# DLRM tower on one core: second layer with samples on partitions, last layer summed along rows by VectorE, narrow products in three of four tiles

## The chip, the core and the metric
One core of a Trainium2 chip. The metric is the device time of one execution in microseconds, as the median of several runs. A measurement of this kernel can tell about 2% from no change.

## What is computed
512 samples. Each has 27 feature vectors of 128 numbers: one dense vector and one row out of each of 26 tables. All 351 products of two different features are formed, and a small network follows.

```python
e = stack([tbl_f[ids[:, f]] for f in range(26)], axis=1)      # tables of 1000 to 125000 rows
all_emb = concatenate([bottom[:, None, :], e], axis=1)        # 512 x 27 x 128
gram = einsum('bfd,bgd->bfg', all_emb, all_emb)
h = concatenate([gram[:, TRIU_I, TRIU_J], bottom], axis=1)    # 351 + 128 = 479 columns
h = maximum(h @ W_top1 + b_top1, 0)                           # 479 -> 512
h = maximum(h @ W_top2 + b_top2, 0)                           # 512 -> 256
y = h @ W_top3                                                # 256 -> 1
```

## The kernel before
The batch is four tiles of 128 samples, a tile being 32 quads of 4 samples. Every engine runs through one list, `PLAN` (line 129), in order, and semaphores tie the engines together.

**Lookups.** The ten smallest tables are looked up by matmul. VectorE (`make_one_hot`, line 632) and ScalarE (lines 696, 703) build one-hot columns for chunks of 125 rows, and TensorE multiplies the table, split in a high and a low part, by them (lines 426, 428). VectorE compares against ids that TensorE has spread over the partitions (`spread_ids`, line 401) into a pair of PSUM banks; ScalarE reads its ids from an SBUF tile that SyncE fills by a broadcast DMA of 256 KB a table (`load_scalar_ids`, line 361). Fillers on the identity matrix (`WARM_UPS`, lines 554, 559) stand ahead of the first table and behind the first spreading. `lookup_ps` is banks 6 and 7.

**Gathers.** The other 16 tables are fetched by 64 indirect DMAs that GpSimd issues one after another (line 345). TensorE turns each with a transpose (`turn`, line 438), four to a group; VectorE or ScalarE copy the group into `turned` (line 582). `TURNED_BY_LOOKUP` says which groups are turned behind which table, 0 to 10 in all; groups 11 to 16 are in `LATE_ORDER`.

**Products.** The 17 blocks (8 quads each, the last two 6 and 2) are multiplied by `multiply` (line 442). Tile 0 has blocks 0 to 3, tile 1 blocks 4 to 7, tile 2 blocks 8 to 11, tile 3 blocks 12 to 16. For each quad there are two matmuls, one for a pair of samples: 56 stationary columns (2 x 28 slots) by 52 moving columns; the two pairs write to PSUM rows 0 to 55 and 64 to 119. Two of the four 28 x 26 squares of a pair are wanted, the others are cross products of two samples and are copied along. `keep` (line 586) copies a block to `products`, VectorE the even and ScalarE the odd ones. `products` has two buffers, so the keep of the first block of tile 2 or 3 waits until tile 0 or 1 is stored.

**The way through DRAM.** SyncE's queue stores a part's products by `store_part` (4 DMAs) and reads them back by `load_part` (7 DMAs) as `pairs`, with the pairs on partitions. The order on the queue is store 0, load 0, store 1, load 1 and so on; each store waits for the keeps, each load for its store. In the last part GpSimd and ScalarE take some of both; ScalarE's two loads stand behind its relus of part 2.

**Layers.** A part has 7 outputs, of 128 columns each. Outputs 0 to 3 are the first layer (`add_dense` line 488, then three `add_pairs` matmuls line 494), 4 and 5 the second (`add_hidden1`, line 501, four matmuls each), 6 the last (`y`, line 508, two matmuls with one stationary column). Features are on partitions throughout. VectorE and ScalarE take them in turn (`take_output`, lines 600 to 615). In the first three parts the outputs alternate between banks 6 and 7. Each fp32 matmul appears in the trace as two instructions, a fp32r matmul or a transpose as one.

`LATE_ORDER` is the order behind the lookups: m is the next block multiplied, t the next group turned, o the next output. With the numbers written out it is now m0 to m8, t11, t12, m9 to m12, o0.0, t13, o0.1 to o0.3, m13, o0.4, t14, o0.5, m14, o0.6, o1.0, t15, o1.1 to o1.4, t16, o1.5, m15, m16, o1.6, o2.0 to o2.6. Then part 3 is done by `layers`.

## Time and profile before
| | us |
|---|---|
| median of 3 runs | 116.31 |
| lowest and highest | 114.5, 116.79 |
| the profiled execution | 113.72 |
| its span, first to last instruction | 111.9 |

The profile is of one execution, so durations and starts are of that one; starts count from the start of the span. PE is TensorE's matmuls, PEld its weight loads, DVE VectorE, ACT ScalarE, POOL GpSimd, SP SyncE; a q behind a name is the queue that issues DMAs. A busy TensorE is not one at its peak, since matmuls overlap: the distance between starts tells more than the duration of one. A mean clock of 0.985 of full speed was granted.

### The profile page before, as it was taken

To read this page: it belongs to the slowest core of one execution; us is meant where nothing else is said; L and a number is where in the kernel's file an instruction comes from. 1 tells how busy PE (TensorE), PEld (TensorE's weight loads), DVE (VectorE), ACT (ScalarE), POOL (GpSimd) and SP (SyncE) were. 2 spreads that over 40 slices of the span, in tenths; PEclk is the share of its full clock that TensorE was granted. 3 is DMA by queue.
4 is the path that set the end of the run, shared out by engine and by line. 5 is a ranking of instruction groups with operands and counts; after the bars stand their busy time and mean duration, and the time that the engine had idled before them with its cause. 6 is when DMAs were issued, how large, how long until landed. Compare 5 with 4: busy or idle time off the path is not lost.

```text
span 111.9 us, 2590 instructions
## 1 busy us (share of the span) xinstructions
PE 103.9 (93%) x1000; PEld 83.7 (75%) x1000; DVE 70.0 (63%) x93; ACT 64.7 (58%) x89; POOL 64.7 (58%) x73
## 2 busy tenths in 40 slices
PE   4969999999999999999998989999869999999892
PEld 4945776868686877766684679998769899897890
DVE  1089999997999999999999144653041512312111
ACT  3386999999999997895952056455214132321111
POOL 2677777776877776777767777777763000212000
PEclk9995799999999999999999999999999999999999
DMA  2899999999998978997322122644646110132000
GB/s 43 243 278 250 215 256 251 252 241 278 242 291 180 261 208 234 278 270 192 92 59 47 51 66 53 151 114 103 191 104 183 41 38 0 33 104 52 14 0 1
DMA packets 10237, 16.67 MB, mean 149 GB/s; under 512 B 5091, under 2 KB 5618, under 8 KB 10225
## 3 DMA queue, kind: packets, MB, share of 16 engines
q1 hardware_dynamic: 7648, 12.03, 42.0%
q0 software_dynamic: 2144, 4.30, 15.3%
q10 hardware_dynamic: 433, 0.18, 0.8%
q8 instruction: 8, 0.13, 0.5%
q14 instruction: 4, 0.03, 0.2%
HBM read 15.01 MB, written 1.49 MB: 147 GB/s over the span
## 4 chain that ended last, share of the span: by engine, by line
PE 31%; DVE 23%; issue 13%; DMA 13%; POOL 10%; SPq 5%; ACT 2%; POOLq 0%; ACTq 0%; DVEq 0%
DVE one_hot L632 17%; POOL mixed_sb L345 10%; PE banks L494 9%; PE banks L501 6%; PE banks L456 6%; DVE low L646 5%; DMA mixed_sb<-in_mixed_table,mixed_rows_sb 5%; DMA products_dram<-products 4%; SPq L318 3%; PE banks L488 3%; PE banks L426 2%; SPq L330 2%; DMA starts_sb<-in_starts 2%; PE banks L428 2%; DMA pairs<-products_dram 2%
## 5 line engine op out<-in xcount | busy, mean ns | idle before, releaser
L345 POOL DMA_INDIRECT mixed_sb<-in_mixed_table,mixed_rows_sb x64 | 62.3, 973 | 21.2 <-issue 19.2
L632 DVE TENSOR_SCALAR one_hot<-banks,starts_sb 125x1024 fp32r<-125x1024 f32 (+1 forms) x44 | 43.8, 1036 | 3.8 <-PE banks L401 3.1
L426 PE MATMUL banks<-one_hot,high 125*128 125x512 f32 x68 | 29.5, 433 | 1.6 <-DVE low L646 1.0
L428 PE MATMUL banks<-one_hot,low 125*128 125x512 f32 x68 | 27.6, 406 | 0.0
L426 PEld LDWEIGHTS banks<-one_hot,high 125*128 125x128 f32 x68 | 13.2, 194 | 11.0 <-DVE one_hot L632 4.0
L708 ACT COPY turned<-banks 128x512 f32<-128x512 f32 x10 | 10.7, 1075 | 9.2 <-PE banks L428 9.1
L678 ACT ACTIVATE hidden<-banks,b_sb 128x128 f32<-128x128 f32 x12 | 4.4, 368 | 19.1 <-PE banks L494 12.8
L428 PEld LDWEIGHTS banks<-one_hot,low 125*128 125x128 f32 x68 | 13.3, 195 | 2.2
L620 DVE TENSOR_SCALAR hidden<-banks,b_sb 128x128 f32<-128x128 f32 x12 | 4.2, 348 | 17.1 <-PE banks L494 11.0
L646 DVE TENSOR_TENSOR low<-raw,high 125x512 fp32r<-125x512 f32 (+1 forms) x20 | 14.7, 736 | 0.0
L456 PE MATMUL banks<-turned 128*56 128x52 f32 x512 | 14.3, 215 | 0.5 <-ACT turned L708 0.5
L456 PEld LDWEIGHTS banks<-turned 128*56 128x56 f32 x512 | 13.7, 132 | 1.2 <-issue 0.8
L596 DVE COPY products<-banks 120x416 f32<-120x416 f32 (+1 forms) x9 | 7.4, 824 | 11.1 <-PE banks L456 5.9
L494 PE MATMUL banks<-pairs,w_sb 128*128 128x128 f32 (+2 forms) x96 | 13.0, 276 | 1.1 <-DMA pairs<-products_dram 1.1
L696 ACT ACTIVATE distance<-lookup_ids_sb,starts_sb 125x512 f32<-125x512 int32 x20 | 13.3, 712 | 0.1
L686 ACT CAST high<-raw 125x1024 fp32r<-125x1024 f32 (+2 forms) x11 | 11.5, 1054 | 2.4 <-DMA raw<-in_tbl 2.4
L494 PEld LDWEIGHTS banks<-pairs,w_sb 128*128 128x128 f32 (+2 forms) x96 | 11.7, 191 | 1.4 <-DMA pairs<-products_dram 1.4
L596 ACT COPY products<-banks 120x416 f32<-120x416 f32 (+1 forms) x8 | 7.0, 870 | 7.5 <-PE banks L456 6.0
L703 ACT ACTIVATE scalar_one_hot<-distance 125x1024 fp32r<-125x1024 f32 x10 | 10.6, 1060 | 0.3
L438 PE MATMUL banks<-identity,mixed_sb 128*128 128x128 f32 x64 | 9.6, 274 | 0.2 <-DMA mixed_sb<-in_mixed_table,mixed_rows_sb 0.2
L582 ACT COPY turned<-banks 128x512 f32<-128x512 f32 (+1 forms) x13 | 7.8, 607 | 3.0 <-PE banks L438 3.0
L438 PEld LDWEIGHTS banks<-identity,mixed_sb 128*128 128x128 f32 x64 | 7.7, 141 | 1.7 <-DMA mixed_sb<-in_mixed_table,mixed_rows_sb 0.4
(32 smaller groups left out, 82.0 us busy)
## 6 DMA issues: line engine op xcount, KB each, us to landing
raw<-in_tbl SPq DMA_DIRECT2D x6, 448.0 KB
lookup_ids_sb<-in_lookup_ids SPq DMA_DIRECT2D x10, 256.0 KB, 6.8
raw<-in_tbl SPq DMA_DIRECT2D x4, 560.0 KB
products_dram<-products SPq DMA_DIRECT2D x14, 91.0 KB
mixed_sb<-in_mixed_table,mixed_rows_sb POOLq DMA_INDIRECT x64, 5.7
pairs<-products_dram SPq DMA_DIRECT2D x15, 39.0 KB
w_sb<-in_w SPq DMA_DIRECT2D x2, 256.0 KB
w_sb<-in_w SPq DMA_DIRECT2D x1, 512.0 KB, 13.9
```

The source lines that it names most:

```text
L345: pool.indirect_dma_start(mixed_sb[:, n, :], None, mixed_table, bass.IndirectOffsetOnAxis(ap=mixed_rows_sb[:, n:n + 1], axis=0),).then_inc ...
L426: pe.matmul(lookup_ps[:, i % 2, :], high[0:TABLE_PARTS, i % 2, c, :], columns, start=(c == 0), stop=False)
L428: last = pe.matmul(lookup_ps[:, i % 2, :], low[0:TABLE_PARTS, i % 2, c, :], columns, start=False, stop=(c == CHUNKS_OF[i] - 1))
L438: last = pe.transpose(turn_ps[:, n % 2, k, :], source, identity[:])
L456: last = pe.matmul(product_ps[rows, b % len(PRODUCT_BANKS), k, 0:PAIR * OTHERS], turned[:, t, q, samples, :].rearrange("p j f -> p (j f)") ...
L494: last = pe.matmul(out(n).rearrange("h (j q) -> h j q", j=QUAD), w1_sb[0:rows, c, h * P:(h + 1) * P], pairs[0:rows, p, :, c, :], start=Fal ...
L596: copy(products[:, t % 2, :, :, quads].rearrange("p j g q -> p q (j g)"), product_ps[0:HALF_END, b % len(PRODUCT_BANKS), 0:quads.stop - qu ...
L632: dve.tensor_scalar(one_hot[0:TABLE_PARTS, n % ONE_HOT_RING:n % ONE_HOT_RING + once, :], banks[0:TABLE_PARTS, first:first + once, :], floa ...
L646: dve.tensor_tensor(low[0:TABLE_PARTS, i % 2, chunks, :], raw[0:TABLE_PARTS, i % RAW_RING, chunks, :], high[0:TABLE_PARTS, i % 2, chunks, ...
L686: act.copy(high[0:TABLE_PARTS, i % 2, chunks, :], raw[0:TABLE_PARTS, i % RAW_RING, chunks, :]).then_inc(high_set, 1)
L696: act.activation(distance[0:TABLE_PARTS, k, :], lookup_ids_sb[0:TABLE_PARTS, i % RAW_RING, :], ACT.Square, bias=starts_sb[0:TABLE_PARTS, F ...
L708: act.copy(turned[:, :, :, :, FIRST_LOOKUP + i].rearrange("p t q j -> p t j q"), lookup_ps[:, i % 2, :].rearrange("p (t j q) -> p t j q", ...
```

## The change
- `add_hidden1` is turned round: hidden1 (128 features by 128 samples) is stationary, and all 256 columns of w2 move. One output of 256 columns takes the place of two of 128; samples are on partitions, features along the row. A part has 5 outputs instead of 7.
- The last layer has no matmul any more. VectorE adds b2 along the row (from PSUM), then one `scalar_tensor_tensor` takes the maximum with 0, multiplies by w3 and sums the row into a column of `y_sb`. For that b2 and w3 are loaded broadcast over all partitions. The output is 128 rows of 4.
- Outputs 0, 2 and 4 of a part are VectorE's, 1 and 3 ScalarE's.
- In tiles 0, 2 and 3 each sample of a quad is a matmul of its own: 28 stationary by 26 moving columns, the four samples at PSUM rows 0, 32, 64 and 96. The keep there copies 124 rows of 26 columns a quad instead of 120 rows of 52.
- Fillers: 5 and 4 instead of 8 and 2.
- ScalarE's ids for the first table come from one more spreading matmul in bank 7; their broadcast DMA is gone.
- Group 1 is turned behind table 1, with group 0, instead of behind table 2.
- The new late order, written out: m0 to m4, t11, m5 to m8, t12, m9 to m12, o0.0 to o0.4, t13, o1.0 to o1.3, t14, t15, m13, t16, m14, m15, m16, o1.4, o2.0 to o2.4.

```diff
-WARM_UPS = (8, 2)
+WARM_UPS = (5, 4)
...
+SAMPLE_START = 32
+PRODUCT_ROWS = (QUAD - 1) * SAMPLE_START + SLOTS
+SINGLE_TILES = {0, 2, 3}
...
-LATE_ORDER = "mmmmmmmmmttmmmmotooomotomootooootommoooooooo"
-TURNED_BY_LOOKUP = {1: 0, 2: 2, 3: 3, 4: 4, 5: 5, 6: 6, 7: 7, 8: 8, 9: 10}
+LATE_ORDER = "mmmmmtmmmmtmmmmoooootoooottmtmmmoooooo"
+TURNED_BY_LOOKUP = {1: 1, 2: 2, 3: 3, 4: 4, 5: 5, 6: 6, 7: 7, 8: 8, 9: 10}
...
+def taker(n):
+    return n % OUTS % 2
...
-            load_scalar_ids(0)
...
-            sp.dma_start(w3_sb[:], w3).then_inc(small_in, 16)
+            sp.dma_start(w3_sb[:], w3.to_broadcast([P, HIDDEN2])).then_inc(small_in, 16)
...
-            sp.dma_start(b2_sb[:], b2).then_inc(small_in, 16)
+            sp.dma_start(b2_sb[:], b2.to_broadcast([P, HIDDEN2])).then_inc(small_in, 16)
...
-                    for h in range(HALVES):
+                    for j in range(QUAD) if t in SINGLE_TILES else []:
+                        last = pe.matmul(product_ps[sample_rows(t, j), b % len(PRODUCT_BANKS), k, 0:OTHERS],
+                                         turned[:, t, q, j, :], turned[:, t, q, j, 1:FEATURES],
+                                         start=True, stop=True)
+                    for h in [] if t in SINGLE_TILES else range(HALVES):
...
-                return pe.matmul(out(n), w2_sb[:, c, h * P:(h + 1) * P], hidden1[:, c, 0:width(p)],
+                return pe.matmul(banks[:, bank_of(n), 0:HIDDEN2], hidden1[:, c, :], w2_sb[:, c, :],
                                  start=(c == 0), stop=(c == OUTS1 - 1))
...
+            pe.matmul(lookup_ps[0:TABLE_PARTS, 1, :], ids_rows[:, BATCH:BATCH + 1].to_broadcast([ID_ROWS, TABLE_PARTS]),
+                      ids_rows[:, 0:BATCH], start=True, stop=True).then_inc(first_ids_spread, 1)
...
+            if t in SINGLE_TILES:
+                copy(products[:, t % 2, 0, :, quads].rearrange("p g q -> p q g"),
+                     product_ps[0:PRODUCT_ROWS, b % len(PRODUCT_BANKS), 0:quads.stop - quads.start, 0:OTHERS]
+                     ).then_inc(kept[which], 1)
+                return
...
+            if p >= 1:
+                eng.wait_ge(y_set, p)
+            eng.tensor_tensor(hidden2[:], banks[:, bank_of(n), 0:HIDDEN2], b2_sb[:], ALU.add
+                              ).then_inc(layer_taken[which], 1)
+            eng.wait_ge(layer_taken[which], takes(n))
+            eng.scalar_tensor_tensor(weighted[:], hidden2[:], 0.0, w3_sb[:], ALU.max, ALU.mult,
+                                     accum_out=y_sb[:, p:p + 1]).then_inc(y_set, 1)
...
-    out = nc.dram_tensor("out_y", (1, BATCH), F32, kind="ExternalOutput").ap()
+    out = nc.dram_tensor("out_y", (P, TILES), F32, kind="ExternalOutput").ap()
```

## Rows read from the trace of the kernel before
**Rows 1.** The page: busy time, share of the span and instructions of each engine.
```profile
PE 103.9 (93%) x1000; PEld 83.7 (75%) x1000; DVE 70.0 (63%) x93; ACT 64.7 (58%) x89; POOL 64.7 (58%) x73
```

**Rows 2.** Busy time by stretches (columns: span, busy us PE, PEld, DVE, ACT, POOL; clock, DMA share, GB/s).
```profile
8.95:12.36 3.41, 3.35 (x9) 1.98 (x8) 3.41 (x5) 2.44 (x4) 2.58 (x3) 0.50 1.04 237
...
77.61:82.07 4.46, 2.76 (x24) 2.37 (x20) 1.03 (x2) 1.18 (x3) 3.49 (x4) 1.00 0.49 142
82.07:102.00 19.93, 19.93 (x240) 18.79 (x240) 5.11 (x13) 4.86 (x11) 3.96 (x6) 1.00 0.29 74
```

**Rows 3.** The timeline (start us, duration us, engine, line): product matmuls.
```profile
65.57 7.65 PE L456 MATMUL banks<-turned 128*56 128x52 f32 x288 [0.46 <-ACT turned L708]
```

**Rows 4.** The timeline: SyncE's queue, stores and loads of the parts.
```profile
70.09 1.63 SPq L318 DMA_DIRECT2D products_dram<-products  x4
...
73.58 2.65 SPq L330 DMA_DIRECT2D pairs<-products_dram  x7
```

**Rows 5.** The timeline: what waited between 78 and 83 us, and the last keep.
```profile
78.86 0.94 PE L494 MATMUL banks<-pairs,w_sb 128*128 128x128 f32 x6 [0.76 <-DMA pairs<-products_dram]
...
80.99 0.85 DVE L596 COPY products<-banks 120x416 f32<-120x416 f32 x1 [4.01 <-DMA products_dram<-products]
...
82.07 0.49 PE L488 MATMUL banks<-dense_turned,w_sb 128*128 128x128 f32 x2 [0.94 <-DVE hidden L620]
...
96.05 0.34 DVE L596 COPY products<-banks 120x104 f32<-120x104 f32 x1 [0.62 <-PE banks L456]
```

**Rows 6.** The groups of instructions by line and form (after the bar: busy us, mean ns).
```profile
L456 PEld LDWEIGHTS banks<-turned 128*56 128x56 f32 x512 | 13.7, 132 | 1.2 <-issue 0.8
...
L646 DVE TENSOR_TENSOR low<-raw,high 125x512 fp32r<-125x512 f32 x12 | 8.2, 681 | 0.0
...
L596 DVE COPY products<-banks 120x416 f32<-120x416 f32 x8 | 7.1, 884 | 10.5 <-PE banks L456 5.3 <-DMA products_dram<-products 5.2
L646 DVE TENSOR_TENSOR low<-raw,high 125x640 fp32r<-125x640 f32 x8 | 6.5, 817 | 0.0
...
L494 PEld LDWEIGHTS banks<-pairs,w_sb 128*128 128x128 f32 x32 | 4.8, 191 | 1.4 <-DMA pairs<-products_dram 1.4
...
L620 DVE TENSOR_SCALAR hidden<-banks,b_sb 128x128 f32<-128x128 f32 x12 | 4.2, 348 | 17.1 <-PE banks L494 11.0 <-PE banks L501 6.1
...
L508 PE MATMUL banks<-hidden,w_sb 128*1 128x128 f32 x16 | 2.6, 271 | 0.5 <-ACT hidden L678 0.3
```

**Rows 7.** The timeline: the tail, from the last loads to the output.
```profile
102.23 0.76 ACTq L330 DMA_DIRECT2D pairs<-products_dram  x2
...
102.90 0.97 PEld L488 LDWEIGHTS banks<-dense_turned,w_sb 128*128 128x128 f32 x8 [0.22 <-issue]
...
104.36 2.75 PEld L494 LDWEIGHTS banks<-pairs,w_sb 128*128 128x128 f32 x24 [0.49 <-DMA pairs<-products_dram]
...
109.42 0.60 PE L508 MATMUL banks<-hidden,w_sb 128*1 128x128 f32 x4 [0.33 <-ACT hidden L678]
...
110.34 0.24 SPq L392 DMA_DIRECT2D out_y<-y_sb  x1
```

**Rows 8.** The timeline: the front; the last line is line 345's time to landing.
```profile
5.15 1.35 PE L401 MATMUL banks<-ids_rows 11*125 11x512 f32 x4
...
12.93 0.95 POOL L345 DMA_INDIRECT mixed_sb<-in_mixed_table,mixed_rows_sb  x1 [0.31 <-issue]
...
18.22 0.60 PE L438 MATMUL banks<-identity,mixed_sb 128*128 128x128 f32 x4
...
23.20 0.60 PE L438 MATMUL banks<-identity,mixed_sb 128*128 128x128 f32 x4
...
24.00 0.66 PE L438 MATMUL banks<-identity,mixed_sb 128*128 128x128 f32 x4 [0.20 <-DMA mixed_sb<-in_mixed_table,mixed_rows_sb]
...
26.57 1.28 DVE L632 TENSOR_SCALAR one_hot<-banks,starts_sb 125x1024 fp32r<-125x1024 f32 x1 [0.70 <-PE banks L428]
...
DMA to landing us min/median/max: 2.5/5.7/8.6
```

More of the change, by code:

```diff
@@ L166, in kept_by, with takes @@
     return (blocks + 1 - which) // 2
-def layer_turns(n):
-    return n // 2 + 1
+def taker(n):
+    return n % OUTS % 2
+def takes(n):
+    return [taker(m) for m in range(n + 1)].count(taker(n))
 def bank_of(n):
@@ L388, in _ @@
                 load_part(sp, p, sync_loads(p), pairs_in[p])
-            for which in range(2):
-                n = len(PARTS) * OUTS - 1 - which
-                sp.wait_ge(layer_taken[n % 2], layer_turns(n))
+            sp.wait_ge(y_set, len(PARTS))
             sp.dma_start(out, y_sb[:]).then_inc(y_stored, 16)
@@ L459, in multiply, with out @@
                 last.then_inc(block_multiplied, 1)
-            def out(n, rows=P):
-                return banks[0:rows, bank_of(n), 0:width(n // OUTS)]
+            def out(n):
+                return banks[:, bank_of(n), 0:width(n // OUTS)]
             def open_bank(n):
                 if bank_user(n) is not None:
-                    pe.wait_ge(layer_taken[bank_user(n) % 2], layer_turns(bank_user(n)))
+                    pe.wait_ge(layer_taken[taker(bank_user(n))], takes(bank_user(n)))
                 elif bank_of(n) in TURN_BANKS:
@@ L474, in await_taken @@
             def await_taken(n):
-                pe.wait_ge(layer_taken[n % 2], layer_turns(n))
+                pe.wait_ge(layer_taken[taker(n)], takes(n))
             def await_pairs(p):
@@ L498, in add_hidden1 @@
             def add_hidden1(n, c):
-                p, k = divmod(n, OUTS)
-                h = k - OUTS1
-                return pe.matmul(out(n), w2_sb[:, c, h * P:(h + 1) * P], hidden1[:, c, 0:width(p)],
+                return pe.matmul(banks[:, bank_of(n), 0:HIDDEN2], hidden1[:, c, :], w2_sb[:, c, :],
                                  start=(c == 0), stop=(c == OUTS1 - 1))
-            def y(n):
-                p = n // OUTS
-                for c in range(OUTS2):
-                    await_taken(p * OUTS + OUTS1 + c)
-                    last = pe.matmul(out(n, 1), w3_sb[:, c:c + 1], hidden2[:, c, 0:width(p)],
-                                     start=(c == 0), stop=(c == OUTS2 - 1))
-                return last
             def output(n):
@@ L523, in output @@
                         last = add_hidden1(n, c)
-                else:
-                    last = y(n)
                 last.then_inc(layer_done, 1)
@@ L538, in layers @@
                     add_pairs(n).then_inc(layer_done, 1)
-                for n in range(first + OUTS1, first + OUTS1 + OUTS2):
-                    open_bank(n)
-                    for c in range(OUTS1 - 1):
-                        await_taken(first + c)
-                        add_hidden1(n, c)
-                await_taken(first + OUTS1 - 1)
-                for n in range(first + OUTS1, first + OUTS1 + OUTS2):
-                    add_hidden1(n, OUTS1 - 1).then_inc(layer_done, 1)
-                open_bank(first + OUTS - 1)
-                y(first + OUTS - 1).then_inc(layer_done, 1)
+                n = first + OUTS1
+                open_bank(n)
+                for c in range(OUTS1):
+                    await_taken(first + c)
+                    last = add_hidden1(n, c)
+                last.then_inc(layer_done, 1)
             pe.wait_ge(identity_set, 1)
@@ L595, in keep, with take_output @@
             quads = quads_of(b)
-            copy(products[:, t % 2, :, :, quads].rearrange("p j g q -> p q (j g)"),
+            if t in SINGLE_TILES:
+                copy(products[:, t % 2, 0, :, quads].rearrange("p g q -> p q g"),
+                     product_ps[0:PRODUCT_ROWS, b % len(PRODUCT_BANKS), 0:quads.stop - quads.start, 0:OTHERS]
+                     ).then_inc(kept[which], 1)
+                return
+            copy(products[0:HALF_END, t % 2, :, :, quads].rearrange("p j g q -> p q (j g)"),
                  product_ps[0:HALF_END, b % len(PRODUCT_BANKS), 0:quads.stop - quads.start, 0:PAIR * OTHERS]
                  ).then_inc(kept[which], 1)
-        def take_output(copy, relu, eng, which, n):
-            if n % 2 != which:
+        def take_output(relu, eng, which, n):
+            if taker(n) != which:
                 return
@@ L739, in _ @@
                         act.wait_ge(small_in, 16 * 3)
-                    take_output(act.copy, relu, act, 1, n)
+                    take_output(relu, act, 1, n)
                 else:
@@ L743, in _ @@
                     for k in range(OUTS):
-                        take_output(act.copy, relu, act, 1, n * OUTS + k)
+                        take_output(relu, act, 1, n * OUTS + k)
 def kernel(**inputs):
@@ L789 @@
         arg("starts", starts), arg("w1", w1), arg("b1", columns(inputs["b_top1"])),
-        arg("w2", inputs["W_top2"]), arg("b2", columns(inputs["b_top2"])),
-        arg("w3", columns(inputs["W_top3"])), out)
+        arg("w2", inputs["W_top2"]), arg("b2", np.asarray(inputs["b_top2"]).reshape(1, HIDDEN2)),
+        arg("w3", np.asarray(inputs["W_top3"]).reshape(1, HIDDEN2)), out)
     result = run_bass_kernel_spmd(nc, [arrays], core_ids=[0])
-    return np.asarray(result.results[0]["out_y"]).reshape(BATCH, 1)
+    return np.asarray(result.results[0]["out_y"]).T.reshape(BATCH, 1)
```

51 lines of the change are left out of this document (26 added, 25 removed).

## Prediction
> **What bounds the kernel now.** The page's busy shares come first: TensorE is busy 93% of a 111.9 us span [rows 1]. "Busy" does not yet say that it sets the end, so the chain of waits is read next, and it has three regimes. Until about 64 us it runs through VectorE's one-hot building; TensorE waits for it there and a cheaper matmul would bring nothing. From the first product matmul at 65.57 us to 82.07 us the chain leaves TensorE and goes keep, store, load: the four blocks of tile 0 are multiplied, kept, written out by SyncE's queue and read back [rows 3, 4]. In the table by stretches TensorE is busy for only 2.76 of the 4.46 us from 77.61 to 82.07 us, and fully busy in the 19.93 us after [rows 2]: there every instruction taken off its queue is time. The tail (last pairs at 104.36, end 111.9) is one dependent chain [rows 7].
>
> **Narrow products.** A block of 8 quads is now 32 recorded matmuls. 288 of them, nine blocks, fill 7.65 us [rows 3]: 0.85 us a block, 26 ns each, 104 ns a quad. What makes the 26 ns? A load of 56 columns lasts 132 ns, of 128 columns 191: (191 - 132)/72 = 0.82 ns a column, 46 ns for 56, 105 for 128 [rows 6]. The halves use different columns of the array, so two instructions share a round of 52 ns, which is 46 and a few more. A narrow product loads 28 columns (23 ns) and moves 26 instead of 52. If the four samples' column groups run side by side as the two halves do, a round of four takes about 23 + 6 = 29 ns, and a quad (two rounds, as each fp32 matmul is recorded twice) 58 ns. If an instruction can't follow another in under 26 ns whatever its width, the quad's 8 take 208 ns. The trace has no row with four groups; these are the two ends. I take 60 ns, near the lower end, because load length plus 6 ns explains both spacings of now: 46 + 6 = 52 here, and 105 + 6 = 111 for 128 columns (24 loads in 2.75 us [rows 7], less the last's 0.19, by 23). So a narrow block is 0.48 us, and with the same small waits 0.50, 0.35 less than a wide one. Tiles 0, 2 and 3 have blocks 0 to 3 and 8 to 16.
> The keep copies halve from 416 to 208 columns. VectorE takes 884 ns for 416 and 341 for 104 [rows 5, 6], 1.74 ns a column, so 0.52 us instead of 0.88; ScalarE about the same.
>
> The Trainium skill speaks against this step: TensorE: Matmul & The Clock Gate, section "Wait — 56ns, not 53.3ns?", says that starts never come closer than about 25 ns however few the columns, and the present 26 ns would sit just on that floor; the same page's "Packing small matmuls" has starts in different tiles 4 ns apart. By the first the quad would cost some 200 ns, by the second what I took. No row here separates them.
>
> **Second layer.** Today 16 instructions of 128 moving columns at 0.111 us (1.78 us), then 4 for the last layer (0.60 us with their latency, plus a wait of about 0.2). After: 4 matmuls of 256 columns, 8 recorded instructions. The last layer's one-column weights do not shorten its spacing ((0.60 - 0.27)/3 = 0.11 [rows 6, 7]), so 128 moving columns cost 0.11 and 256 cost 0.22: 8 x 0.22 = 1.75 us. Each part saves about 0.7 us of TensorE. VectorE gets a PSUM addition over 256 columns: 0.35 for the 128-column relu plus 128 x 1.06 ns (from 681 ns at 512 and 817 at 640 columns) = 0.48 us. Then comes a multiply with a row sum: at least 0.68 - 0.27 = 0.41 (the 512-column subtraction less half of its columns) and, if the summing took a pass of its own, 0.85; I take 0.5 [rows 6]. Both are hidden behind other matmuls in parts 0 to 2, where VectorE has 5.11 busy of 19.93 us [rows 2]; in part 3 they are exposed.
>
> **The order after 65.57 us.**
> 1. Blocks 0 to 3 are done 4 x 0.35 = 1.4 us sooner and the last keep is 0.4 shorter. Tile 0's stores start at 68.3 instead of 70.09, the loads land at 77.1 instead of 78.8 [rows 4, 5].
> 2. Nine of the thirteen blocks before the first output are narrow: 9 x 0.35 = 3.1 us, TensorE reaches it at about 74.5 instead of 77.6. But it must wait there for step 1's pairs until 77.1: of 3.1 us, 1.7 arrive.
> 3. VectorE's keep of block 12 stands ahead of its relus and waits until tile 1 is stored; today that holds VectorE 4.01 us and TensorE 0.94 [rows 5]. Those stores are behind tile 0's seven loads on SP (2.65 us [rows 4]), so they too come 1.7 us sooner, at about 79.3, and no more. Output 0.2 starts at about 80.35, not 82.07.
> 4. From there TensorE is the bound. Left: outputs 0.2 and 0.3 and the eight of parts 1 and 2, 10 x 8 x 0.111 = 8.9; three second layers 5.2; turns 13 to 16 (12 transposes and their waits) 1.55; blocks 13 to 16, 24 quads at 0.06 and their waits, 1.6. Sum 17.3, end 97.6; today the queue is there at 102.90 [rows 7], so 5.3 us are gained.
> 5. ScalarE issues its two last loads only after its last relu of part 2. Today they are issued at 102.23 and in use at 104.36 [rows 7]; that relu becomes output 2.3, some 96.5, so they land at 98.6. TensorE's four dense products fill the time until then. The last pairs start at 98.65 instead of 104.36: 5.7 us sooner. The last blocks are kept near 91 instead of 96.4 [rows 5], so the stores are ready before that.
> 6. Tail: pairs 24 x 0.111 = 2.7 (101.35); the relu of the last, 0.25 + 0.35 + 0.1, lies behind the first three second-layer steps (1.3); second layer ends 103.1, visible 103.4; VectorE 0.48 + 0.06 + 0.5 (104.5); the output 1.56 as from 110.34 to 111.9, plus 0.2 for 128 short rows in place of one. End 106.2.
>
> **The front.** Three fewer fillers at first can bring the first spreading of the ids forward (5.15 now [rows 8]), by some tenths. What that gives is lost again: turn 1 now follows table 1. Its last gather starts at 12.93, takes 0.95, lands 5.7 later (median), 19.6 [rows 8]; TensorE is free at 18.66 (four transposes from 18.22) and waits. Table 2 is then delayed by about 1 + 0.45 us and ends at 23.2 + 1.45 = 24.65 (turn 1 starts at 23.20 now); turn 2 follows, done near 25.1 instead of 24.45. VectorE waits for that part of the chain once (0.70 at 26.57 [rows 8]), and its chain sets all until 64 us: 0.5 to 0.65 late. Against this, one 256 KB broadcast is gone, at 237 GB/s 1.1 us of a saturated stream (share 1.04 [rows 2]); the gathers may land up to that much sooner. Together -0.2 to +0.8; I take +0.3. The broadcast w3 and b2 (128 KB each) are wanted 20 us after they are issued, at a DMA share under 0.5: nothing.
>
> **Sum.** 106.2 + 0.3 = 106.5, against a span of 111.9: -5.4 us. The profiled execution took 113.72 us in all, 1.8 around its span, and lies 2.6 under the median of the three, 116.31. I put the difference on the median: 110.9 us.
>
> **Rivals.**
> A (0.12), slower: the narrow matmuls keep 26 ns each. A block is then 1.66 us and more, and the 96 narrow quads, 12 blocks' worth, cost 12 x 0.83 = 10 us more than wide ones. TensorE waits for nothing any more before step 4 (today about 1.7 us), saves 2.1 in the last layer and is through with part 2 at 102.9 + 10 - 1.7 - 2.1 = 109.1; with 0.9 for the dense products, 7.5 for pairs to end and 0 for the front that is a span of 117.5, 121.9 on the median. The floor that the Trainium skill names above would act as this rival. For it: the 26 ns of now; against: the load's length explains the same 26. Between B's 13 ns (109.1) and these 26 (117.5) the end is as before at about 17 ns.
> B (0.13), half of it: the queue delivers an instruction each 13 ns, so a quad costs 104 as now. Step 1 loses 1.4 us, step 4 0.7, and step 2's surplus hides the rest: 106.5 + 2.1 and a few tenths of waits, 109.1, on the median 113.5, 2.4% under before.
> C (0.10), the clock: it stood at half for 3.41 us from 8.95 [rows 2], when TensorE had begun and stopped several times. Step 2 leaves TensorE waiting over 2 us near 75. One such stretch at half speed in step 4 costs 1.7 us: 112.6.
> D (0.05), front: if turn 1 waits for the slowest landing of the trace (8.6 us [rows 8]) it lands at 22.5, 2.9 later than I took: 113.8.
> E (0.05), the transfers do not follow: if tile 1's stores, which cross the gathers, still land at 80.9, step 3's 1.7 us are lost: 112.6.
> The rest, 0.55, is the forecast itself, 108 to 113 with the unknown prices (0.35 for the row sum, 1.0 for the front, the spread of 114.5 to 116.8 in the runs).
>
> **Range and chances.** 107.5 to 115 leaves out A and some 0.03 below and 0.03 between. A measurement of this kernel can tell about 2%, 2.3 us, from no change. Faster by over 2% (below 114.0): the forecast, B for the greater part, C and half of D, 0.75; within: 0.12; slower: A and a trifle, 0.13.
>
> **What would show it.** Spacing of the narrow matmuls: 8 ns or less confirms, 26 is A, 13 is B. Tile 0's stores near 68.3; a TensorE wait of about 2 us for pairs near 75; VectorE's block-12 keep still waiting for tile 1's store; the last pairs starting near 98.9; two VectorE instructions of about 0.5 us at the end; a TensorE wait of 1 us for gathers near 19. Wrong it would be if the instructions that have doubled in number and not their columns set the pace.

## The result, and the profile after

The changed kernel takes 119.36 us (median; 118.99 to 119.91), the kernel before 115.41 us beside it on the same chip: ratio 1.045, interval 1.037 to 1.052. It is slower by 4 us in the medians where 5.4 less were forecast. The ratios with an interval, here and below, compare the fast executions of both kernels alone, and two of the four of the kernel before were slow ones that lift its median. The profiled execution took 118.99 us around a span of 117.2.

The page: busy share of each engine; its row of tenths of the granted clock; the instruction queue (packets, MB, share); and the group of the narrow products (after the bar: busy us, mean ns of one, idle time before them).
```profile
PE 102.3 (87%) x1335; PEld 81.9 (70%) x1335; DVE 69.8 (60%) x99; ACT 60.4 (52%) x83; POOL 63.6 (54%) x73
PEclk9999999999999999999999999999977999999999
q8 instruction: 10, 0.16, 0.5%
L462 PE MATMUL banks<-turned 128*28 128x26 f32 x768 | 10.5, 192 | 7.3 <-issue 6.3
```
[Rows 1] had TensorE busy 93% of 111.9 us. It is now busy 1.6 us less, in a span 5.3 us longer: it stands still more, and what ended the standing is "issue", which says that nothing the profile shows did, no semaphore and no transfer. All its waits from 64 to 110 us (total, times, longest):
```profile
PE banks L462 <- issue: 6.3, 4, 2.3
PE banks L446 <- issue: 1.3, 1, 1.3
PE banks L462 <- ACT turned L718: 0.4, 1, 0.4
PE banks L468 <- issue: 0.4, 1, 0.4
```
Nothing is left of the waits for pairs and for VectorE that [rows 5] showed; 8.0 us of "issue" stand in their place. The timeline of TensorE shows where (start, duration, then in brackets the idle time before):
```profile
65.74 3.04 PE L462 MATMUL banks<-turned 128*28 128x26 f32 x201 [0.44 <-ACT turned L718]
69.72 0.66 PE L462 MATMUL banks<-turned 128*28 128x26 f32 x55 [0.94 <-issue]
...
73.42 1.80 PE L468 MATMUL banks<-turned 128*56 128x52 f32 x61 [0.43 <-issue]
...
77.73 0.49 PE L446 MATMUL banks<-identity,mixed_sb 128*128 128x128 f32 x3 [1.29 <-issue]
...
81.40 1.93 PE L462 MATMUL banks<-turned 128*28 128x26 f32 x127 [1.35 <-issue]
85.62 0.25 PE L462 MATMUL banks<-turned 128*28 128x26 f32 x5 [2.29 <-issue]
...
97.73 0.74 PE L462 MATMUL banks<-turned 128*28 128x26 f32 x64
...
101.46 0.48 PE L462 MATMUL banks<-turned 128*28 128x26 f32 x30 [1.76 <-issue]
```
The stops fall in the middle of a block (201 + 55 matmuls are four blocks), of a group of four transposes (1 + 3), of the wide block of tile 1. No `wait_ge` stands in such a place. They last 0.4 to 2.3 us, and each comes after a whole number of blocks of 256 instructions, as the count below shows. Where there is no stop the pace is near the 7.5 ns that was forecast: the block at 97.73 takes (0.74 - 0.19)/63 = 8.7 ns a matmul.

**Counting the instructions.** I numbered TensorE's instructions in the trace, weight loads and multiplies alike, and wrote down when certain numbers begin. A star marks a stop ended by "issue". e1 to e5 are experiments of the next section.
```
            start of TensorE's instruction number (us)
            707     963     1219    1475    1731    1987    2243    2499
before     67.44   70.70   74.89   82.73   91.82  103.78
after      66.35   69.72*  73.42*  77.76*  81.40*  85.62*  98.05  101.47*
e1 wide    68.72   72.59   76.69   85.29   94.70
e2         67.76   71.69*  75.40   79.62*  83.83*  87.76*  97.71  105.12
e3         66.45   70.09*  74.61   78.49   85.85   95.27
e4         68.20   72.07   75.95   79.55*  91.24   95.02*
e5         67.42   71.07*  74.90*  80.60   84.32*  88.54*  98.29  102.38
```
(A stop ends within two or three numbers of the column's. No stop marks the columns without a star; they are counted on, and may be some tens of instructions off: in e5 the packet for the block behind 2243 starts at 96.61, before the 98.29 counted, and in the kernel before one starts at 80.64, before the 82.73.) All stars of the kernel after lie whole multiples of 256 instructions apart. The queue of instructions on the page carries packets of 16,384 bytes, 256 instructions of 64 bytes: ten of them here, and TensorE passes ten such numbers (195, 451, 707 and so on); in the kernel before it is eight and eight, in e1 seven and seven, in e5 eleven and eleven. For each of these stops the trace has one packet, with much the same rhythm:
```
new 256 entered   packet starts   packet takes   next 256 begins   from entry to next
    66.35             67.27           0.88            69.72              3.37
    69.72             71.08           0.88            73.42              3.70
    73.42             75.29           1.05            77.76              4.34
    77.76             79.11           0.93            81.40              3.64
    81.40             83.21           0.92            85.62              4.22
    98.05             98.78           1.25           101.47              3.42
```
The fetch of the next 256 starts 0.7 to 1.9 us after TensorE has entered the present ones, takes 0.9 to 1.25, and they can run 1.4 to 1.6 us after it has landed. TensorE gets at most 256 instructions in 3.4 to 4.3 us, 13 to 17 ns each, so 26 to 34 ns for a matmul with its load. Wide products need 26.5 ns [rows 3], at the edge of that: the kernels with wide fp32 products alone stop for 0 to 0.6 us, at number 1219 only. Narrow ones want 8.7 and run dry. What delays a packet by 0.7 to 1.9 us is not shown; no run changes the DMA traffic beside it.

The Trainium skill, Runtime: NRT & Kernel Launch, section "Instruction fetch mechanics", has blocks of 256 instructions fetched while the present ones run, at a cost "mostly hidden". On the 256 the trace agrees; on the cost it does not. The section also gives TensorE's store as 2048 instructions and, further down, as two lines of 256; the trace (and e4 below) fits only the second. The measurement decides.

### The profile page after: what moved, and what is told of

The parts are those of the page before. It is cut to its first block, busy times and chain, and to the rows that moved or that the text cites. A ratio compares the mean times of both kernels' runs of the same rounds, so it can differ in the third digit from the quotient of the medians.

```text
span 117.2 us, 3253 instructions
## 1 busy us (share of the span) xinstructions
PE 102.3 (87%) x1335; PEld 81.9 (70%) x1335; DVE 69.8 (60%) x99; ACT 60.4 (52%) x83; POOL 63.6 (54%) x73
## 4 chain that ended last, share of the span: by engine, by line
PE 39%; DVE 25%; issue 19%; DMA 7%; POOL 6%; ACT 1%; POOLq 0%; DVEq 0%
DVE one_hot L638 18%; PE banks L506 10%; PE banks L462 9%; DVE low L652 6%; POOL mixed_sb L356 6%; PE banks L512 6%; DMA mixed_sb<-in_mixed_table,mixed_rows_sb 5%; PE banks L500 4%; PE banks L468 3%; PE banks L446 3%; PE banks L434 2%; DMA starts_sb<-in_starts 2%; PE banks L436 2%; ACT turned L718 1%; PE banks L409 1%
## 5 line engine op out<-in xcount | busy, mean ns | idle before, releaser
L356 POOL DMA_INDIRECT mixed_sb<-in_mixed_table,mixed_rows_sb x64 | 61.1, 955 | 21.3 <-issue 19.2
L462 PE MATMUL banks<-turned 128*28 128x26 f32 x768 | 10.5, 192 | 7.3 <-issue 6.3
L718 ACT COPY turned<-banks 128x512 f32<-128x512 f32 x10 | 10.7, 1067 | 10.0 <-PE banks L436 9.9
L462 PEld LDWEIGHTS banks<-turned 128*28 128x28 f32 x768 | 8.8, 105 | 9.3 <-issue 8.9
L506 PE MATMUL banks<-pairs,w_sb 128*128 128x128 f32 (+2 forms) x96 | 14.2, 293 | 0.0
L684 ACT ACTIVATE hidden<-banks,b_sb 128x128 f32<-128x128 f32 x8 | 2.9, 368 | 19.9 <-PE banks L506 19.9
L506 PEld LDWEIGHTS banks<-pairs,w_sb 128*128 128x128 f32 (+2 forms) x96 | 13.1, 209 | 0.0
L706 ACT ACTIVATE distance<-lookup_ids_sb,starts_sb 125x512 f32<-125x512 int32 x18 | 12.0, 712 | 0.5 <-DMA lookup_ids_sb<-in_lookup_ids 0.5
L329 POOL DMA_DIRECT2D products_dram<-products x1 | 0.6, 573 | 19.1 <-DVE products L596 19.1
L596 DVE COPY products<-banks 124x208 f32<-124x208 f32 (+1 forms) x7 | 3.3, 473 | 12.0 <-PE banks L462 12.0
L596 ACT COPY products<-banks 124x208 f32<-124x208 f32 (+1 forms) x6 | 3.0, 507 | 13.4 <-PE banks L462 13.4
```

Of the source, the lines that this page charges most:

```text
L356: pool.indirect_dma_start(mixed_sb[:, n, :], None, mixed_table, bass.IndirectOffsetOnAxis(ap=mixed_rows_sb[:, n:n + 1], axis=0),).then_inc ...
L462: last = pe.matmul(product_ps[sample_rows(t, j), b % len(PRODUCT_BANKS), k, 0:OTHERS], turned[:, t, q, j, :], turned[:, t, q, j, 1:FEATURE ...
L506: last = pe.matmul(out(n).rearrange("h (j q) -> h j q", j=QUAD), w1_sb[0:rows, c, h * P:(h + 1) * P], pairs[0:rows, p, :, c, :], start=Fal ...
L706: act.activation(distance[0:TABLE_PARTS, k, :], ids, ACT.Square, bias=starts_sb[0:TABLE_PARTS, FIRST_START + n:FIRST_START + n + 1]).then_ ...
L718: act.copy(turned[:, :, :, :, FIRST_LOOKUP + i].rearrange("p t q j -> p t j q"), lookup_ps[:, i % 2, :].rearrange("p (t j q) -> p t j q", ...
```

## The experiments

All times are beside the kernel before on the same chip. "From the first product" is the span's end less the start of the first product matmul, which keeps the front's scatter of about 1 us out: 46.3 us before, 51.5 after.

**e1, all products wide**: the rest of the change without the narrow products.
```diff
-SINGLE_TILES = {0, 2, 3}
+SINGLE_TILES = set()
```


> The changed kernel with every tile's products wide again (56 by 52 columns); second layer, row sum, late order, fillers and first ids as changed. Theory S (supply): in the changed kernel's trace the narrow matmuls start 8 ns apart in bursts, but TensorE stands still after every 256 of its instructions (before instructions 963, 1219, 1474, 1730, 1986, 2498 of its stream), because a block of 256 instructions is used up faster than the next one arrives, one per 3.8 to 4.2 us. Wide, 768 matmul and load instructions fewer, the stops vanish and the span is 109 us (my forecast of 106.5 plus 2.1 for the wide blocks and a few tenths), time about 113. Theory L (the second layer turned round, with VectorE's two steps, costs the time): the span stays above 114. Theory C (the half-clock stretch at 86.3 to 89.7 us is the loss): it vanishes too, but brings only 1.7 us if the stops were harmless.

Measured: 113.27 us, ratio 0.980 (0.967 to 0.994), span 110.9, 44.1 from the first product. TensorE's waits after 64 us:
```profile
PE banks L500 <- DVE hidden L626: 1.5, 1, 1.5
PE banks L506 <- DMA pairs<-products_dram: 0.8, 1, 0.8
PE banks L468 <- ACT turned L718: 0.4, 1, 0.4
```
No "issue", and the two waits of [rows 5] are back. (A stop of the supply too short for this list is there: at 76.68, number 1219, two matmuls start 0.22 us apart.) So everything but the narrow products gains about 2%, and they lose 7.4 us from the first product (51.5 - 44.1). The gain lies behind the waits: output 0.2 starts 17.3 us after the first product in e1 and 16.5 before, and from there to the end it is 26.9 us against 29.8.

**e2, narrow products alone**: the kernel before with `sample_rows`, `multiply` and the keep of the change, nothing else.
```diff
+SINGLE_TILES = {0, 2, 3}
...
+                    for j in range(QUAD) if t in SINGLE_TILES else []:
+                        last = pe.matmul(product_ps[sample_rows(t, j), b % len(PRODUCT_BANKS), k, 0:OTHERS],
+                                         turned[:, t, q, j, :], turned[:, t, q, j, 1:FEATURES],
```


> The kernel before with nothing changed but the narrow products in tiles 0, 2 and 3. Theory S: 768 more instructions for TensorE behind 65.6 us, some 2290 in all, nine blocks at about 3.9 us; stops of 1 to 2 us in the products, span 119 to 121 us, ratio to the kernel before 1.06 to 1.08. Theory L: without the new second layer the narrow products bring their 3 us, span 109 to 110.

Measured: 122.99 us, ratio 1.057 (1.044 to 1.070), a little under the 1.06 expected, with 5.8 us of "issue" stops and a mean clock of 0.944. The loss belongs to the narrow products and needs nothing else of the change.

**e3, only tile 0 narrow.**
```diff
+SINGLE_TILES = {0}
```


> The changed kernel with narrow products in tile 0 alone. Theory S: some 400 instructions (one and a half blocks) are at hand when the products begin and are used up in 3 us; one stop of about 1 us comes in block 3 or 4, after which the supply keeps up with the wide blocks. Tile 0's stores start between 69.5 and 71.5, no earlier than with wide products; span within 1 us of the all-wide kernel, 109 to 110. If the narrow matmuls themselves were slow (26 ns each) the stores would start at 73 and the span be 112 or more.

Measured: 113.15 us, ratio 0.977 (0.967 to 0.988), span 111.5, 45.7 from the first product; one of the four executions took 238.62 us, for a reason that nothing here shows. Its stop, and its first store beside that of the kernel after and of e1:
```profile
65.84 2.99 PE L462 MATMUL banks<-turned 128*28 128x26 f32 x201 [0.45 <-ACT turned L718]
70.09 0.86 PE L462 MATMUL banks<-turned 128*28 128x26 f32 x55 [1.25 <-issue]
```
```profile
71.80 1.62 SPq L329 DMA_DIRECT2D products_dram<-products  x4
```
```profile
71.57 1.64 SPq L329 DMA_DIRECT2D products_dram<-products  x4
```
```profile
71.32 1.62 SPq L329 DMA_DIRECT2D products_dram<-products  x4
```
Counted from the first product the stores start after 5.96 us (e3), 5.83 (after) and 4.51 (e1, all wide). Four narrow blocks are later, not 1.4 us sooner, and the store misses the 71.5 expected by 0.3. The whole times of e3 and e1 can't be told apart. Counted from the first product e3 takes 1.5 us more: the stop is made good by the wait for pairs, which is gone, but the clock stood at half from 70.42 to 73.83, right behind the stop.

**e5, the same kernel with 128 more instructions early.** If a stop comes with the number of the instruction, it must move when others are put ahead of it; if it comes from the block, its banks or its copies, it must not.
```diff
             spread_ids(1)
+            for _ in range(32):
+                pe.matmul(turn_ps[0:1, 0, 0, 0:1], identity[:, 0:1], identity[:, 0:1], start=True, stop=True)
```


> The changed kernel with 32 tiny fp32 matmuls (one column, one moving column; 128 recorded instructions) more behind the second spreading of the ids, long before the products. If the stops belong to the places in the instruction stream (theory S), they come at the same counts of TensorE instructions as before (963, 1219, 1474 and so on), so 128 instructions, a narrow block, earlier in the work: the first in block 2 instead of block 3. If they belong to something in the work (a bank, a wait for a copy or a store), they stay at the same matmuls and the counts grow by 128.

Measured once: 122.23 us, span 120.5. The stops:
```profile
71.07 1.71 PE L462 MATMUL banks<-turned 128*28 128x26 f32 x119 [1.84 <-issue]
74.89 1.37 PE L468 MATMUL banks<-turned 128*56 128x52 f32 x24 [1.56 <-issue]
84.32 1.72 PE L462 MATMUL banks<-turned 128*28 128x26 f32 x127 [1.33 <-issue]
88.53 0.93 PE L462 MATMUL banks<-turned 128*28 128x26 f32 x68 [2.50 <-issue]
```
The first stop comes after (961 - 687)/2 = 137 narrow matmuls instead of 201, in block 2 instead of 3: 64 matmuls, 128 instructions, sooner. The numbers 963, 1219, 1731 and 1987 stayed. The span says nothing, from one execution; the places of the stops decide between the supply and everything that hangs on a block.

**e4, only tile 3 narrow**: is more than one block of 256 held after a long slow stretch?
```diff
+SINGLE_TILES = {3}
```


> The changed kernel with narrow products in tile 3 alone (blocks 12 to 16). These stand among matmuls of 110 ns and more, which use 256 instructions in some 12 us or more, so the next blocks of instructions are at hand. Theory S: no stop, or one short one if the supply of two blocks runs out within the 380 instructions of blocks 13 to 16; TensorE gets through these blocks about 1.1 us sooner than wide, span 0 to 1.5 us under the all-wide kernel's, counted from the first product (44.1 us there). A floor of 26 ns an instruction would make it 4.2 us longer.

Measured: 114.99 us in the median against 115.53; the executions of the two kernels overlap, and no interval is given (taken like the other ratios it is about 0.99, from two executions). Missed: not at most one short stop, but two, and 46.0 us from the first product where at most 44.1 were expected; the clock stood at half from 95.01 to 98.43, behind the second stop.
```profile
79.55 0.25 PE L462 MATMUL banks<-turned 128*28 128x26 f32 x5 [0.82 <-issue]
...
95.02 0.58 PE L462 MATMUL banks<-turned 128*28 128x26 f32 x30 [2.12 <-issue]
```
From 79.55 to 91.24 (the second counted) TensorE worked through one block of 256 in 11.7 us, time for about three fetches. Yet the packet for number 1987 starts only at 92.61, 11.4 us after the one before it (81.25) and 1.4 us after 1731 was entered, and the stop, 2.12 us, is longer than five of the six of the kernel after. Time saved up on slow instructions does not count: one block ahead is held, no more.

**e6, wide products with as many instructions as narrow ones**: a product of one element ahead of each wide one in tiles 0, 2 and 3, into a place that nobody reads.
```diff
+                        if t != 1:
+                            pe.matmul(product_ps[h * HALF_START:h * HALF_START + 1, b % len(PRODUCT_BANKS), k, 56:57],
+                                      turned[:, t, q, 0, 1:2], turned[:, t, q, 0, 1:2], start=True, stop=True)
```


> All products wide, but in tiles 0, 2 and 3 each is preceded by a tiny fp32 matmul (one stationary, one moving column, into an unused PSUM column), so that TensorE's stream is as long as with narrow products; the output is not touched. Theory S: what costs is the number of instructions, not that they are narrow: stops after each 256 instructions come back, at the same counts, and the span rises from the all-wide 110.9 to 116 to 120. If the stops come from writing four groups of PSUM rows or from narrow weights, this kernel has none, and costs only what the tiny matmuls take to execute, at most 10 us if each takes 25 ns and 1 to 3 us if they lie beside the wide ones.

Measured: 192.33 us, ratio 1.676 (1.661 to 1.692), span 190.1. Missed, and it can't tell the theories apart, since it costs something else. A stretch of its timeline:
```profile
89.72 0.43 PE L471 MATMUL banks<-turned 128*56 128x52 f32 x2
90.08 0.19 PE L469 MATMUL banks<-turned 128*1 128x1 f32 x2
90.20 0.43 PE L471 MATMUL banks<-turned 128*56 128x52 f32 x2
```
A pair of wide and a pair of tiny matmuls take 0.48 us; two wide ones alone take 0.053 [rows 3] at full clock. Over the run it is (190.1 - 110.9)/384 = 0.21 us for each of the 384 tiny ones; part of that is the clock, 0.59 in the mean from 75 to 150 us. So alternating the two shapes costs by itself far more than the supply. The Trainium skill, TensorEngine Tiling (Array Packing), section "Key Properties", says that a change of the tiling mode drains TensorE; it names no price, and this run fits it without proving it, as shape and mode change together.

**e8 and e10, wide products in other orders**: is the new late order to blame or to praise? Both are e1 with another `LATE_ORDER`; e10's is the order of before, with 5 outputs a part.
```diff
-LATE_ORDER = "mmmmmtmmmmtmmmmoooootoooottmtmmmoooooo"
+LATE_ORDER = "mmmmmmmmmttmmmoomtoomotmotooootmmooooo"
```


> As the last, but block 12 moved behind output 0.1. VectorE's keep of block 12, which waits for the store of tile 1, then no longer stands ahead of its relu of output 0.0, and TensorE has block 12 and turn 13 to do while that store is on its way. In the all-wide kernel TensorE stood still 1.5 us there. Expected: that wait gone, the wait for the first pairs 0.8 us longer, 0.5 to 1 us less in all: from the first product 43.0 to 43.6 us.

```diff
-LATE_ORDER = "mmmmmtmmmmtmmmmoooootoooottmtmmmoooooo"
+LATE_ORDER = "mmmmmmmmmttmmmmotooomotmotooootmmooooo"
```

> All products wide, second layer as changed, but the late order as in the kernel before (its outputs 5 and 6 struck out), so that blocks 13 and 14 and turns 13 to 15 stand between the outputs. TensorE is the bound from about 84 us on in the all-wide kernel, and its work is the same in any order; what can be gained is the filling of its waits for pairs (0.8 us) and for VectorE's held relu (1.5 us) with turn 13, 0.5 us. Span from the first product 43.3 to 44.1 us (all-wide: 44.1).

Measured: e8 114.42 us, ratio 0.984 (0.975 to 0.992), 46.2 from the first product; e10 114.02 us, ratio 0.987 (0.981 to 0.994), 44.9. e8 missed its 43.0 to 43.6, and e10 its 43.3 to 44.1. e8 waits 1.4 us for pairs and 1.5 for late turns, and even it has a stop of the supply (number 1219), after 317 wide matmuls with only eight transposes between them:
```profile
75.50 1.99 PE L468 MATMUL banks<-turned 128*56 128x52 f32 x67 [0.62 <-issue]
```
Over all executions the three orders can't be told apart (ratios 0.980, 0.984 and 0.987 with intervals that overlap); in the profiled ones e1's is 0.8 us shorter than e10's and 2.1 shorter than e8's.

**e7 and e11, bf16 products, narrow and wide**: a bf16 matmul is recorded once, not twice, so the same narrow products are half the instructions. Both multiply rounded values, so the products are less exact.
```diff
-        turned = sb("turned", [P, TILES, QUADS, QUAD, SLOTS])
+        turned = sb("turned", [P, TILES, QUADS, QUAD, SLOTS], BF16)
```


> The changed kernel, narrow in tiles 0, 2 and 3, with the tile that the products are made from held in bf16, so that the products are of rounded values (this part of the computation is less exact). A bf16 matmul is one recorded instruction and one load instead of two and two: a narrow block has 64 instructions instead of 128, as a wide fp32 one has. Theory S: four narrow blocks lie in 256 instructions; blocks 0 to 8 have some 540 instructions instead of 960; at least three of the five stops behind 69 us vanish and the sum of the stops falls from 8.8 us to under 2.5; span 104 to 108. If narrow matmuls in four groups were themselves the trouble, the stops or a pace of 26 ns would stay: a narrow block at 0.8 us or more.

> The same bf16 tile with all products wide (32 instructions a block). The partner of the last run: with instructions enough, narrow and wide can be compared for what they cost in the array and in the keep copies. Theory S together with my forecast of the copies: narrow is 0 to 2 us faster than wide, since its keeps are 0.36 us shorter and blocks no longer; if narrow is slower by 1 us or more even here, something else than the supply speaks against it.

Measured: e7 119.06 us, ratio 1.036 (1.028 to 1.046), span 115.8; e11 116.44, ratio 1.009 (1.001 to 1.017), span 114.2. e7 missed its span of 104 to 108, from a cause at the front: ScalarE's copy of the looked-up rows into `turned` writes bf16 and takes 2,576 ns instead of 1,067 for fp32 to the same places.
```profile
L719 ACT CAST turned<-banks 128x512 bf16<-128x512 f32 x10 | 25.8, 2576 | 1.9 <-PE banks L437 1.9
```
The first product starts at 73.17 and 73.83. From there e7 takes 42.6 us and e11 40.4. e7 has one stop of the supply (1.7 us at 81.57, number 1219) where the kernel after had six: halving the instructions took most stops away, as expected. That narrow is still 2.2 us slower than wide, where it was to be up to 2 faster, is not settled by it: e7 had 13.7 us at half clock behind its first product and e11 10.2, and the difference of 3.4 us is worth up to 1.7; e7 also has short stops in its bursts, some 0.9 us in all, of which e11 has next to none. Between stops a narrow bf16 block takes as long as a wide one: 32 matmuls of 6.9 ns against 16 of 14.4.

**e9, wide products and the front of before**: what do the fillers and the earlier turn 1 cost?
```diff
-WARM_UPS = (5, 4)
+WARM_UPS = (8, 2)
...
-TURNED_BY_LOOKUP = {1: 1, 2: 2, 3: 3, 4: 4, 5: 5, 6: 6, 7: 7, 8: 8, 9: 10}
+TURNED_BY_LOOKUP = {1: 0, 2: 2, 3: 3, 4: 4, 5: 5, 6: 6, 7: 7, 8: 8, 9: 10}
```


> The all-wide kernel with the fillers (8 and 2) and turn 1's place (behind table 2) of the kernel before; only the first ids still come from TensorE. This prices the front. The starts of the first product so far: 65.57 in the kernel before, 65.74, 65.84, 66.81 and 66.29 with the new front, and 67.17 in the kernel before with narrow products alone, whose front is the old one. Theory F (the new front costs, as I forecast, 0.3 us on the median): ratio to the kernel before lower than the all-wide kernel's 0.980 by 0.002 to 0.006. Rival: the start of the products scatters by a microsecond from execution to execution with the landing of gathers, and the ratio is the same within its interval.

Measured: 113.24 us against 115.17, 0.983 by the medians (no interval is given; taken like e1's 0.980 it is about 0.975, from two executions), span 110.3, first product at 65.73, 44.6 us from there. In the profiles with the new front it starts between 65.30 and 66.81, with the old between 65.57 and 67.17 (e5 and the bf16 pair left out). The ratio would fit theory F, but two executions and e1's interval can't tell it from none, and from the first product e9 is no faster. No difference of the front is shown.

**e12, wide products, block 12 later**: in e1 VectorE's keep of block 12 waits for tile 1's store and holds its relus up (1.52 us of TensorE at 84.07). Here block 12 follows behind outputs 0.0 and 0.1.
```diff
-LATE_ORDER = "mmmmmtmmmmtmmmmoooootoooottmtmmmoooooo"
+LATE_ORDER = "mmmmmtmmmmtmmmoomoootoooottmtmmmoooooo"
```


> The all-wide kernel with block 12 moved behind output 0.1 and nothing else. In the all-wide kernel VectorE's keep of block 12 stood ahead of its relu of output 0.0 and waited 4.04 us for the store of tile 1, and TensorE stood still 1.52 us for that relu. Now TensorE should get outputs 0.0 and 0.1 as soon as the first pairs land and do block 12 while the store finishes: output 0.2 starts 0.7 us sooner after the first product (17.3 us there), the end 0.7 us sooner (44.1 there). Ratio to the kernel before 0.975, if the span of the front does not differ; it is a candidate for the fastest exact version. Rival: the wait only moves to the pairs (0.81 us there, 1.6 here), and nothing is gained.

Measured: 113.16 us, ratio 0.975 (0.965 to 0.986), span 111.0, 45.5 from the first product. The ratio is the one expected, but not by the way expected: the wait for VectorE is gone, while that for pairs has grown from 0.8 to 1.9 us, the clock is at half behind it, and output 0.2 starts 18.6 us after the first product instead of 16.6:
```profile
79.90 1.65 PE L506 MATMUL banks<-pairs,w_sb 128*128 128x128 f32 x6 [1.89 <-DMA pairs<-products_dram]
```
e1, e3, e9 and e12 can't be told from each other; all are about 2% faster than the kernel before, none by clearly more than a measurement can tell, and about 6% faster than the change (0.98 against 1.045).

## Why the prediction was wrong

**The step that failed is "Narrow products".** It worked out what the array needs for a quad and asked whether an instruction could follow the other fast enough; it never asked whether the instructions would be there. The pace of the array was right: 8.7 ns a matmul measured, 7.5 forecast. The 26 ns of [rows 3] fit the load's length, as the prediction said, though columns loaded and columns moved were halved together and no run parts them. There is no floor at 26: what the Trainium skill says of 25 ns (TensorE: Matmul & The Clock Gate, "Wait — 56ns, not 53.3ns?") as the least distance between starts does not hold between different column groups of this kernel. But each of the twelve blocks' worth of narrow products has 128 instructions, loads counted, where a wide one has 64: 768 more, 2743 of TensorE's instead of e1's 1975 (before: 2081). Number 1987 is passed at 85.62 in the kernel after; e1 has not as many in its whole span. e5 and the packets show that the supply makes the stops, and e1 that they go with the narrow products.

The account from the first product, e1 to after:
```
e1, all wide                                                     44.1
its waits for pairs and VectorE, gone                            -2.3
12 narrow blocks of 64 x 8.7 ns = 0.56 instead of 0.85 us        -3.5
six stops, start to start: 1.13 0.64 1.56 1.54 2.19 1.95         +9.0
ten short stops inside the bursts, 0.20 to 0.29 us each          +2.5
half clock from 86.27 to 89.68                                   +1.7
sum                                                              51.5
measured                                                         51.5
```
A stop counts here from start to start, some 0.2 us more than the idle time in brackets, since a matmul's own time runs out first; the fifth is 2.19 and not 2.29 + 0.2, since its bracket takes in the short stop just ahead of it, which is counted in the next line. The short stops can be seen in the weight loads of the first four blocks (timeline, PEld):
```profile
65.91 1.15 PEld L462 LDWEIGHTS banks<-turned 128*28 128x28 f32 x89
67.20 0.63 PEld L462 LDWEIGHTS banks<-turned 128*28 128x28 f32 x58 [0.15 <-issue]
68.00 0.28 PEld L462 LDWEIGHTS banks<-turned 128*28 128x28 f32 x18 [0.17 <-issue]
68.46 0.20 PEld L462 LDWEIGHTS banks<-turned 128*28 128x28 f32 x11 [0.19 <-issue]
69.72 0.55 PEld L462 LDWEIGHTS banks<-turned 128*28 128x28 f32 x55 [1.05 <-issue]
```
They are no block of 256: the first falls 185 instructions after the first product both here and in e5, where all numbers are 128 higher. What they are stays open. That the sum meets the measurement to a tenth is partly luck; each of its terms is good to a few tenths.

**Point by point.**
- *Spacing.* Forecast 8 ns or less: 8.7 within a burst, so B's queue (13) and A's floor (26) are not there. Over a stretch the supply makes it 26 to 34.
- *Step 1.* Stores at 68.3: they started at 71.57. In e3 too the gain of 1.4 us became a loss.
- *Step 2.* TensorE was to wait 2 us for pairs near 75. It never waited for pairs; it reached them at 86.15, not 77.1. The wait is real where TensorE comes to it early: 0.81 us in e1, 1.89 in e12.
- *Step 3.* The keep of block 12 was to wait for tile 1's store. It waited 3.72 us for TensorE instead (85.91). In e1 the wait is there, 4.04 us of VectorE and 1.52 of TensorE.
- *Step 4.* What is not product was sized well: an output of the first layer 0.89 us (from 93.30 to 94.19), a second layer of 8 instructions 1.73 (forecast 1.75).
- *Step 5.* ScalarE's loads left at 107.54, right behind its relu at 107.48 (forecast 96.5), and TensorE went on to the last pairs without a wait, at 109.90 instead of 98.65. The order of things was right, some 11 us late.
- *Step 6.* The tail from the last pairs at 109.90 to 117.2 is 7.3 us (7.55). In it VectorE's addition took 0.42 (0.48) and the row sum 0.42 + 0.08 (0.5):
```profile
112.58 1.89 PE L512 MATMUL banks<-w_sb,hidden 128*128 128x256 f32 x8
...
114.51 0.42 DVE L617 TENSOR_TENSOR hidden<-banks,b_sb 128x256 f32<-128x256 f32 x1 [2.04 <-PE banks L512]
114.97 0.42 DVE L620 SCALAR_TENSOR_TENSOR weighted<-hidden,w_sb 128x256 f32<-128x256 f32 x1
115.32 0.08 DVE L620 DVE_READ_ACCUMULATOR weighted<-hidden,w_sb 128x1 f32 x1
115.43 0.36 SPq L400 DMA_DIRECT2D out_y<-y_sb  x1
```
- *Keep.* 0.51 us for 208 columns (0.52).
- *Front.* Forecast +0.3, with 1 us of waiting for gathers near 19; the wait was 0.49 at 19.24 and the first product came at 65.74 instead of 65.57.
- *Rival C.* The half clock came, where the forecast had it at 0.10 and at the price it gave, 1.7 us: 1.2 GHz for 3.41 us, right behind the stop of 2.29.
```profile
65.74:85.86 20.12, 13.27 (x713) 11.25 (x713) 4.80 (x8) 4.62 (x8) 13.74 (x15) 1.00 0.40 107
86.27:89.68 3.41, 3.41 (x19) 3.41 (x18) 0.51 (x2) 0.35 (x1) 0.00 (x0) 0.50 0.41 92
```
(Stretch, span, busy us of PE, PEld, DVE, ACT, POOL, clock, DMA share, GB/s.) TensorE is busy 13.27 of the first 20.12 us, where it was to be saturated but for 2.
- *Rival A.* It gave a span of 117.5, measured 117.2. The price was right because 26 ns for each matmul is close to what the supply delivers (26 to 34); the mechanism was wrong, and with it the chance of 0.12, which was taken from the array's behaviour alone. The prediction's last sentence named what happened, instructions and not columns setting the pace, but no term and no chance stood behind it. The row for one existed, on the page of before, and was not used:
```profile
q8 instruction: 8, 0.13, 0.5%
```
TensorE's 2081 instructions by these 8 packets are 260 each, and 0.13 MB by 8 are 16 KB.

With wide products the forecast for the rest was too good as well: e1's span is 110.9 where its expectation had 109, of which about 0.9 us are its later first product (66.81 against 65.57 and the 0.3 forecast); the rest of the miss stays open.

## What to carry to other kernels

Splitting a matmul to use the array better multiplies TensorE's instructions. Before doing so, count the instructions, loads too, in the densest stretch: here 256 of them cost 3.4 to 4.3 us however short they were, so a shape that needs less than 13 ns an instruction gains nothing beyond the first one or two blocks of 256. A busy TensorE that turns into "issue" idle time in the middle of a loop without waits, at multiples of 256 instructions, is that limit; fewer and wider matmuls are the cure, or long ones in between within each block, and never more than one block's worth is saved up.

## What the runs showed of the hardware

- TensorE's instructions come in packets of 16 KB, 256 instructions (as many packets as blocks in every kernel counted). From entering one block to the start of the next it takes 3.4 to 4.3 us when they run out, and only one block is fetched ahead (e4: the next packet started 11.4 us after the one before it, and TensorE still ran dry for 2.12 us).
- Narrow fp32 matmuls on four column groups start 8.7 ns apart; bursts have further stops of 0.20 to 0.29 us whose cause is open.
- Alternating a 1x1 with a 56x52 matmul costs 0.2 us for each tiny one, half clock included (e6).
- ScalarE's copy of 512 fp32 columns takes 1.07 us into fp32 and 2.58 us into bf16 at the same places (e7).
- Half clock (1.2 GHz) for 3.4 us or more came with or within about 1 us behind TensorE's stops of 2.29 us in the kernel after, 1.25 in e3, 2.12 in e4, 1.84 and 2.50 in e5, and its wait of 1.89 in e12. Behind the other five stops of the kernel after (up to 1.76) and e1's wait of 1.52 it stayed at 2.4 GHz, so the length of one stop alone does not decide it.
